# Layer 0 holds its 192 channels as 128 and 64 instead of 96 and 96

## The chip, the cores and the metric

The kernel runs on one core of one Trainium2 chip. The metric is the device time of one launch in microseconds. The core has TensorE (matmuls, into PSUM), VectorE, ScalarE, GpSimd and SyncE, which issues the DMAs; each has its own queue of instructions, and they wait for one another by semaphores.

## The reference

The input x is 16 images of 56x56 tokens with 192 channels, fp32. Layer 0 is a window attention block and an MLP:

```
xn = layernorm(x) * ln1_w + ln1_b, rolled by (-3, -3), in windows of 7x7 tokens
q, k, v = xn @ qkv_w + qkv_b              # 6 heads of 32 channels, 49 tokens a window
o = softmax(q k^T / sqrt(32)) v           # per window and head
x = x + roll back(o @ proj_w + proj_b)
x = x + gelu(layernorm(x) @ mlp_w1 + mlp_b1) @ mlp_w2 + mlp_b2      # 192 -> 768 -> 192
```

Layer 1 is a selective scan in four directions over the image, with 192 channels and 16 states, and a LayerNorm at the end. The change does not touch it.

## The kernel before

`build` runs four blocks one after the other: `build_layer0`, `build_prep` (projections of the scan), `build_scan` and `build_output`. The change is in `build_layer0` and in the layout of one table of per-channel constants (`cols0`).

Layer 0 works in 128 units. A unit is one row of 8 windows of an image: 8 x 49 = 392 tokens. The loop over units is software pipelined: `step(u)` does the attention of unit u and the MLP of unit u - 1. Each engine has its own program of the step, in a fixed order written out by hand, and waits on semaphores that count units and pieces.

Tokens stand on partitions in two places (x and LayerNorm, in tiles of 98 tokens, `PT`, of which there are four, `NPAIR`); elsewhere channels stand on partitions. The 192 channels are held as two halves of 96 (`HC`), index a, on the partitions 0 to 95: `xnT[96, 2, ...]`, `qkT[96, 4, 392]`, `oT`, `h2T`, `x1T`, and the weights as `[96, 2, ...]`. So each product over channels is two accumulated matmuls of 96 rows with 392 tokens as columns (192 for v and proj).

TensorE's order in `step`:

1. q and k (L436): four pieces of 96 channels into PSUM banks 6 and 7 in turn, each waiting until ScalarE (L336) has copied the piece two before it.
2. LayerNorm 2's transposes of unit u - 1 (L375, `norm2_transposes`), once VectorE has made x-hat (L200). ScalarE applies scale and shift (L289, `affine`).
3. v (L447): four pieces into banks 6 and 7, copied by VectorE (L242).
4. `mlp_in` (L398): six pieces of 128 hidden channels into banks 6 and 7, each followed by a gelu on ScalarE (L306); at the end ScalarE loads its exp table (L308).
5. `pair_scores` (L422): q times k for a pair of windows, 12 matmuls of 32 rows and 49 columns, into banks 0 to 2 or 3 to 5. The pairs 0 and 1 come first, the pairs 2 and 3 after a third of `mlp_out` each. VectorE takes the maximum (L213), subtracts it (L215), and after ScalarE's exp (L345) sums (L221), inverts and scales (L225).
6. `mlp_out` (L407) for the channel half a = 0 in three thirds, with the residual x2 added by an identity matmul (L411).
7. For each pair: transposes of the probabilities (L471) into banks 2 and 3, one third of `mlp_out` for a = 1, and the weighted sums of v (L482) of the pair before. Between them VectorE copies the transposed probabilities to SBUF (L254, L255); the banks are single, so the transposes of the next pair wait for this copy.
8. LayerNorm 1's transposes for the next unit (L375), and after ScalarE's copy of the attention output (L352, `oT`) the projection (L497). VectorE adds the residual (L262, `x2`), which starts LayerNorm 2.

ScalarE's order is: rstd of LayerNorm 2, q and k copies (with the rstd of LayerNorm 1 after the third), `affine` for h2T, six gelus, four exps, `result` (x1T, L319 to L322), `oT`, `affine` for xnT. SyncE loads the next unit's x and stores x1T to the DRAM tensor `scr_x` with one DMA (L144). GpSimd adds the projection's bias to x (L177).

The prep stage, of which the prediction uses rows, computes 192 channels as 128 and 64: two full matmuls (L695), then two of 64 rows, one on the partitions 0 to 63 (L697), one on 64 to 127 (L699), into different banks. The scan sums with two matmuls of 64 columns (L1014) into the two partition halves of one bank.

Of the kernel before, what the change touches and what calls it, by code (L numbers as in the profile page):

```python
# [15 lines left out]
ACT = mybir.ActivationFunctionType  # L16
# [15 lines left out]
NPAIR = UW // 2  # L32
HID = 4 * C
# [19 lines left out]
def build_layer0(nc, io, xn, n_units):  # L53
    x_win, w_qkv, w_proj, w1, w2, cols0, b1c, pb, ident = io
    with ExitStack() as ctx:
# [20 lines left out]
        xnT = sb("xnT", [HC, 2, UW, WP])  # L76
        qkT = sb("qkT", [HC, 4, UT])
# [6 lines left out]
        oT = sb("oT", [HC, 2, UT])  # L84
        x2 = sb("x2", [PT, NPAIR, C])
        h2T = sb("h2T", [HC, 2, UT])
        g_sb = sb("g_sb", [128, MC, UT])
        x1T = sb("x1T", [HC, 2, 2, UT])
# [5 lines left out]
        LN1W, LN1B, QKB, VB, LN2W, LN2B, B2 = 0, 2, 4, 8, 10, 12, 14  # L94
# [12 lines left out]
        s_full = sem("a_s_full")  # L107
# [21 lines left out]
        def _(sp):  # L129
            for dst, src in ((wqkv_sb[:], w_qkv.rearrange("(a p) n -> p a n", a=2)),  # L130
                             (wp_sb[:], w_proj.rearrange("(a p) n -> p a n", a=2)),
                             (w1_sb[:], w1.rearrange("(a p) n -> p a n", a=2)),
                             (w2_sb[:], w2.rearrange("(a p) n -> p a n", a=MC)),
# [27 lines left out]
            def last(u, half, par):  # L161
                sp.wait_ge(x1_done, 2 * u)
                store(u - 1, 1 - par)
                sp.wait_ge(x1_out[0], 16 * half + 16)
                sp.wait_ge(x1_out[1], 16 * half + 16)
# [4 lines left out]
        def _(pool):  # L170
            pool.wait_ge(w_in, 16 * 8)
# [11 lines left out]
        def _(dve):  # L183
            nc.vector.memset(ps[:, 0:6, :], 0.0)
            nc.vector.memset(xnT[:], 0.0)
            nc.vector.memset(eps_sb[:], LN_EPS).then_inc(ready, 1)
# [43 lines left out]
            def step(u, half, par, first, is_last):  # L230
# [1196 lines left out]
```

## Time and profile before

| | us |
|---|---|
| median of 3 runs | 23417.88 |
| lowest and highest run | 23393.66 and 23420.24 |
| the profiled execution | 23412.67 |
| its span | 23410.9 |
| PE busy in the span | 17671.3 (75%) |
| DVE busy | 19513.2 (83%) |
| ACT busy | 9356.7 (40%) |
| POOL busy | 16923.9 (72%) |

Layer 0 takes the first 5360 us of the span, the prep stage lies behind it until about 7850 us, then come the scan and, at the very end, the output. The shares of the whole span are means over these stages: in layer 0 GpSimd does almost nothing, in the scan VectorE and GpSimd are busy nine tenths. In a timeline of the profile neighbouring instructions of one line are merged into one row with their number; a time in brackets is the engine's idle time before the row and what ended it.

### The profile page before, as it was taken

What the parts mean: (1) busy time and instruction counts of PE and PEld (TensorE: products, weight loads), DVE (VectorE), ACT (ScalarE), POOL (GpSimd) and SP (SyncE); (2) the same over time, 40 slices, a digit from 0 to 9 for tenths busy, and PEclk for the clock granted to TensorE, in tenths of its full rate; (3) what the DMA queues carried; (4) which work ended last, traced back from release to release, by engine and by line L of the source; (5) the groups of instructions that cost most, each with busy time, mean ns of one, the idle gap of its engine ahead of it and who ended that gap; (6) DMA issues with size and microseconds to landing.
All of it is one profiled execution on the core that took longest, in us unless ns stands there. A gap on an engine that the chain in (4) does not pass through costs nothing. (4 is left out here: it accounts for less than half of the span.)

```text
span 23410.9 us, 290956 instructions
## 1 busy us (share of the span) xinstructions
PE 17671.3 (75%) x83608; PEld 6368.3 (27%) x83608; DVE 19513.2 (83%) x21619; ACT 9356.7 (40%) x14503; POOL 16923.9 (72%) x9092
## 2 busy tenths in 40 slices
PE   8999999997777677777777777777777777777731
PEld 5556555552222111111111111111111111111111
DVE  5555555556666899999999999999999999999976
ACT  3333333334444344444444444444444444444420
POOL 0000000007888899999999999999999999999977
PEclk9999999998777676777677677767766776677665
DMA  0000000004555555555555555555555555555556
GB/s 17 15 15 14 14 14 14 14 14 148 184 178 181 140 118 121 119 122 117 116 121 122 121 116 118 122 121 120 118 117 120 121 122 117 116 121 122 119 135 166
DMA packets 918185, 2417.28 MB, mean 103 GB/s; under 512 B 61030, under 2 KB 270440, under 8 KB 901680
## 3 DMA queue, kind: packets, MB, share of 16 engines
q1 hardware_dynamic: 917040, 2404.95, 45.2%
q8 instruction: 360, 5.90, 0.1%
q14 instruction: 785, 6.43, 0.1%
HBM read 1897.33 MB, written 507.38 MB: 103 GB/s over the span
## 5 line engine op out<-in xcount | busy, mean ns | idle before, releaser
L1162 POOL TENSOR_TENSOR c_pr<-c_hs,c_c_u 128x784 f32<-128x784 f32 x6144 | 11216.7, 1847 | 749.4 <-DVE c_hs L1126 749.4
L1069 ACT ACTIVATE c_psum<-c_dt_u,c_a_neg 128x784 f32<-128x784 f32 x6144 | 5641.6, 918 | 8506.4 <-DVE c_hs L1126 8458.7
L1014 PE MATMUL c_psum<-c_pr,c_red 128*64 128x392 f32 x24576 | 7519.3, 728 | 0.0
L1126 DVE TENSOR_TENSOR_SCAN c_hs<-c_psum,c_carry,c_dbx 128x784 f32<-128x784 f32 x3456 | 6272.7, 1845 | 0.0
L1003 PE MATMUL c_psum<-c_br_u,c_sel 48*128 48x512 bf16 (+1 forms) x9216 | 3210.5, 441 | 3994.8 <-DVE c_dbx L1106 3888.7
L1106 DVE TENSOR_TENSOR c_dbx<-c_u_u,c_psum 128x784 f32<-128x784 f32 x4608 | 4390.2, 953 | 55.4 <-PE c_psum L1003 55.4
L177 POOL TENSOR_TENSOR a_xpb<-a_x_sb,a_pb_sb 98x768 f32<-98x768 f32 x128 | 231.0, 1804 | 5059.8 <-DVE a_x L262 5048.7
L1151 POOL TENSOR_TENSOR c_dbp<-c_u_u,c_bp_u 128x784 f32<-128x784 f32 x1536 | 2858.7, 1861 | 45.0 <-DMA c_c_u<-scr_bc 45.0
L1003 PEld LDWEIGHTS c_psum<-c_br_u,c_sel 48*128 48x128 bf16 x9216 | 557.3, 102 | 8494.5 <-DVE c_dbx L1106 7963.1
L1014 PEld LDWEIGHTS c_psum<-c_pr,c_red 128*64 128x64 f32 x24576 | 1807.9, 181 | 3522.1 <-issue 2286.9
L1126 DVE TENSOR_TENSOR_SCAN c_hs<-c_psum,c_carry,c_dbp 128x784 f32<-128x784 f32 x1152 | 2133.1, 1852 | 0.0
L1126 DVE TENSOR_TENSOR_SCAN c_hs<-c_psum,c_dbx 128x784 f32<-128x784 f32 x1152 | 2018.9, 1782 | 18.6 <-issue 18.6
L407 PE MATMUL a_psum<-a_g_sb,a_w_sb 128*96 128x392 f32 x3072 | 1165.8, 502 | 0.7 <-ACT a_g_sb L306 0.7
L695 PE MATMUL p_psum<-p_xm,p_wk 128*128 128x392 f32 x1536 | 913.6, 724 | 333.7 <-ACT p_xb L726 323.6
L213 DVE TENSOR_REDUCE a_mx<-a_psum 128x6 f32<-128x294 f32 x512 | 234.2, 457 | 1028.2 <-PE a_psum L422 1028.2
L813 POOL TENSOR_SCALAR p_cap<-p_xb 128x784 f32<-128x784 f32 x384 | 988.7, 2575 | 139.6 <-ACT p_xb L726 106.4
L398 PE MATMUL a_psum<-a_h2T,a_w_sb 96*128 96x392 f32 x3072 | 1045.0, 497 | 20.7 <-DVE a_v_sb L242 16.5
L825 POOL TENSOR_TENSOR p_u_o<-p_dt_o,p_xm 128x784 f32<-128x784 f32 x384 | 786.0, 2047 | 237.8 <-DMA scr_u<-p_u_o 208.6
L436 PE MATMUL a_psum<-a_xnT,a_wqkv_sb 96*96 96x392 f32 x2048 | 748.8, 508 | 90.8 <-ACT a_qkT L336 88.3
L790 DVE SCALAR_TENSOR_TENSOR p_psum<-p_m_t,p_psum 128x784 f32<-128x784 f32 x384 | 375.7, 978 | 509.2 <-ACT p_psum L746 496.6
L254 DVE COPY a_pT<-a_psum 49x384 f32<-49x384 f32 x512 | 280.3, 547 | 617.2 <-PE a_psum L471 617.2
L306 ACT ACTIVATE a_g_sb<-a_psum,a_b_sb 128x392 f32<-128x392 f32 x768 | 450.8, 587 | 766.4 <-PE a_psum L398 766.4
(104 smaller groups left out, 17976.1 us busy)
## 6 DMA issues: line engine op xcount, KB each, us to landing
c_c_u<-scr_bc SPq DMA_DIRECT2D x512, 1568.0 KB, 26.9
c_dt_u<-scr_dt SPq DMA_DIRECT2D x512, 588.0 KB, 7.4
c_u_u<-scr_u SPq DMA_DIRECT2D x512, 588.0 KB, 10.8
c_bp_u<-scr_bc SPq DMA_DIRECT2D x512, 392.0 KB, 20.2
scr_dt<-p_dt_o SPq DMA_DIRECT2D x128, 1176.0 KB, 9.6
scr_u<-p_u_o SPq DMA_DIRECT2D x128, 1176.0 KB, 7.2
scr_y<-c_y_sb SPq DMA_DIRECT2D x256, 294.0 KB, 14.4
d_yin<-scr_y SPq DMA_DIRECT2D x32, 2352.0 KB, 14.4
```

The lines of the kernel that those rows point to most:

```text
L398: mm = pe.matmul(ps[:, 6 + m % 2, 0:UT], w1_sb[:, a, 128 * m:128 * m + 128], h2T[:, a, :], start=(a == 0), stop=(a == 1))
L407: pe.matmul(ps[0:HC, 6 + a, 0:UT], w2_sb[:, m, HC * a:HC * a + HC], g_sb[:, m, :], start=(m == 0), stop=False)
L695: pe.matmul(bank(k, h), wk[:, o, 0, m0:m0 + 128], order(xm[:, par, 0, :], o, c, h, HT), start=True, stop=False)
L813: nc.gpsimd.tensor_scalar(cap[:, j % 2], xb[:, n_of(c, j) % 4], CLAMP, None, ALU.min).then_inc(cap_done, 1)
L825: nc.gpsimd.tensor_tensor(u, dt, order(xm[:, par, k, :], o, c, 0, CT), ALU.mult).then_inc(u_done, 1)
L1003: mm = pe.matmul(b_ps[:, n0:n1], sel[:, s % NPR, :], br_u[:, d, n0:n1], start=True, stop=True)
L1014: mm = pe.matmul(Y(3 * w + q)[64 * h:64 * h + 64, :], red[:], pr[:, s % RP, HT * h:HT * h + HT], start=(p == 0 and opens(w)), stop=(p == N ...
L1069: nc.scalar.activation(dA(s), dt_u[:, d, s // NPR, :], ACT.Exp, scale=a_neg[:, k, s:s + 1]).then_inc(exp_done, 1)
L1106: nc.vector.tensor_tensor(dbx[:, (MULS * w + i) % RB, :], u_u[:, d, s // NPR, :], b_ps, ALU.mult).then_inc(mul_done, 1)
L1126: nc.vector.tensor_tensor_scan(hs[:, s % RH, way], dA(s)[:, way], data, init, ALU.mult, ALU.add).then_inc(scan_done, 1)
L1151: nc.gpsimd.tensor_tensor(dbp[:, (len(POOL_STEPS) * w + i) % RG, :], u_u[:, d, s // NPR, :], bp_u[:, d, POOL_PAIRS.index(s % NPR), :], ALU ...
L1162: nc.gpsimd.tensor_tensor(pr[:, s % RP, :], hs[:, s % RH, :], c_u[:, d, s % NPR, :], ALU.mult).then_inc(prod_done, 1)
```

## The change

The 192 channels are held as 128 and 64. The first 128 stand on all partitions, for 392 tokens. The other 64 stand twice: for tokens 0 to 195 (f = 0) on partitions 0 to 63, for tokens 196 to 391 (f = 1) on partitions 64 to 127; these are the new tiles `xnL`, `qkL`, `oL`, `h2L`, `x1L` of 196 tokens. The last 64 rows of the weights are loaded to both partition halves. Products with 128 channels are written as two matmuls of 196 tokens (f = 0, 1) into two banks, followed by two of 64 rows, one for each partition half. Products that make the other 64 channels write partitions 0 to 63 for f = 0 and 64 to 127 for f = 1 of one bank.

The heads 0 to 3 lie in the first 128 channels, the heads 4 and 5 in the rest. `pair_scores` does the heads 0 to 2, then waits for them by the new semaphore `s_half`, then does the heads 3 to 5. The q and k pieces go to banks 4, 5 and 6, v to banks 2 and 3 at once, `mlp_in` to the bank pairs 6, 4 and 6 (`GATE`) with one signal to ScalarE for two gelus. The transposes of the other 64 channels are plain identity matmuls, two passes each. The store is four DMAs, of which three have short pieces (28, 25 and 3 tokens).

```diff
-LN1W, LN1B, QKB, VB, LN2W, LN2B, B2 = 0, 2, 4, 8, 10, 12, 14
+LN1W, LN1B, QB, KB, VB, LN2W, LN2B, B2 = 0, 2, 4, 6, 8, 10, 12, 14
+part = lambda f: slice(WP * f, WP * f + WP)
+cut = lambda f: slice(UH * f, UH * f + UH)
+halved = lambda bank, k: ps[:, bank:bank + 2, cut(k)]
+GATE = (6, 4, 6)
...
+    for tile, w in ((wqkv_sb, w_qkv), (wp_sb, w_proj), (w1_sb, w1)):
+        sp.dma_start(tile[:, 0, :], w[0:128]).then_inc(w_in, 16)
+        sp.dma_start(tile[0:64, 1, :], w[128:C]).then_inc(w_in, 16)
+        sp.dma_start(tile[64:128, 1, :], w[128:C]).then_inc(w_in, 16)
...
+        dst = xrow[:, bass.ds(u * UT + SHIFT * IMG, UT)]
+        sp.dma_start(dst[0:128], x1T[:, par]).then_inc(x1_out[par], 16)
+        low = dst[128:C].rearrange("p (i c) -> p i c", i=WS)
+        lows = x1L[:, par].rearrange("p (i c) -> p i c", i=WS)
+        mid, end = IMG // 2, IMG // 2 - SHIFT
+        sp.dma_start(low[:, :, SHIFT:SHIFT + mid], lows[0:64]).then_inc(x1_out[par], 16)
+        sp.dma_start(low[:, :, SHIFT + mid:IMG], lows[64:128, :, 0:end]).then_inc(x1_out[par], 16)
+        sp.dma_start(low[:, :, 0:SHIFT], lows[64:128, :, end:mid]).then_inc(x1_out[par], 16)
...
+        dve.wait_ge(v_full, u + 1)
+        if not first:
+            dve.wait_ge(av_full, u)
+        for f in range(2):
             for w in range(2):
+                ins = nc.vector.tensor_copy(v_sb[:, HW * f + w:HW * f + HW:2, :],
+                                            ps[WP * w:WP * w + WT, 2 + f, 0:2 * C].rearrange("p (e c) -> p e c", e=2))
+        ins.then_inc(v_evac, 1)
         if not first:
             dve.wait_ge(pt_full, NPAIR * u)
...
+    def affine(dst, low, bank, wcol, bcol, done):
+        for a, (to, n) in enumerate(((dst, UT), (low, UH))):
+            ins = nc.scalar.activation(to, ps[:, bank + a, 0:n].rearrange("p (w k) -> p w k", k=WT), ACT.Identity,
...
     def gelus(u):
         for m in range(MC):
-            act.wait_ge(h_full, MC * u + m + 1)
-            nc.scalar.activation(g_sb[:, m, :], ps[:, 6 + m % 2, 0:UT], ACT.Gelu,
+            act.wait_ge(h_full, MC // 2 * u + m // 2 + 1)
+            nc.scalar.activation(g_sb[:, m, :].rearrange("p (f t) -> p f t", f=2), halved(GATE[m // 2], m % 2), ACT.Gelu,
                                  bias=b1_sb[:, m:m + 1]).then_inc(gelu_done, 1)
...
+        act.wait_ge(qk_full, 2 * u + 1)
+        if not first:
+            act.wait_ge(s_full, NPAIR * u)
+        for a, col in ((0, QB), (1, KB)):
+            nc.scalar.activation(qkT[:, a, :].rearrange("p (f t) -> p f t", f=2), halved(4, a), ACT.Identity,
+                                 bias=cols[:, col:col + 1]).then_inc(qk_evac, 1)
+        act.wait_ge(qk_full, 2 * u + 2)
+        for a, col in ((0, QB + 1), (1, KB + 1)):
+            nc.scalar.activation(qkL[:, a, :], ps[:, 6, cut(a)], ACT.Identity,
+                                 bias=cols[:, col:col + 1]).then_inc(qk_evac, 1)
+        if not is_last:
+            rstd_of(0, u + 1)
...
     def transposes(which, bank, done):
         for t in range(NPAIR):
+            pe.transpose(ps[:, bank, PT * t:PT * t + PT], xhat[:, which, t, 0:128], id_sb[0:PT, 0:PT])
+        for t in (0, 2, 1, 3):
+            mm = pe.matmul(ps[part(t // 2), bank + 1, PT * (t % 2):PT * (t % 2) + PT], xhat[:, which, t, 128:C],
+                           id_sb[0:PT, 0:PT], start=True, stop=True)
         mm.then_inc(done, 1)
...
     def mlp_in(u, attn_u):
         pe.wait_ge(h2_done, u + 1)
+        for m in range(0, MC, 2):
+            if m == 0:
                 pe.wait_ge(x2_done, 2 * u + 2)
+                if attn_u is not None:
+                    pe.wait_ge(qk_evac, 4 * attn_u + 4)
+            elif m == 4:
+                pe.wait_ge(gelu_done, MC * u + 2)
+            for k in range(2):
+                w = slice(128 * (m + k), 128 * (m + k) + 128)
+                for f in range(2):
+                    pe.matmul(ps[:, GATE[m // 2] + f, cut(k)], w1_sb[:, 0, w], h2T[:, cut(f)], start=True, stop=False)
+                for f in range(2):
+                    mm = pe.matmul(ps[:, GATE[m // 2] + f, cut(k)], w1_sb[part(f), 1, w], h2L[part(f), :],
+                                   start=False, stop=True)
+            mm.then_inc(h_full, 1)
+    def mlp_out(u, a, third):
...
+        if a == 0 and third == 0:
+            pe.wait_ge(gelu_done, MC * u + MC)
+        for m in (2 * third, 2 * third + 1):
+            if a == 0:
+                pe.matmul(ps[:, 6, 0:UT], w2_sb[:, m, 0:128], g_sb[:, m, :], start=(m == 0), stop=False)
             else:
+                for f in range(2):
+                    pe.matmul(ps[part(f), 7, 0:UH], w2_sb[:, m, 128:C], g_sb[:, m, cut(f)], start=(m == 0), stop=False)
+        if third == 2:
+            if a == 0:
+                for t in range(NPAIR):
+                    mm = pe.matmul(ps[:, 6, PT * t:PT * t + PT], x2[:, t, 0:128], id_sb[0:PT, 0:PT],
+                                   start=False, stop=(t == NPAIR - 1))
+            else:
+                for t in (0, 2, 1, 3):
+                    mm = pe.matmul(ps[part(t // 2), 7, PT * (t % 2):PT * (t % 2) + PT], x2[:, t, 128:C],
+                                   id_sb[0:PT, 0:PT], start=False, stop=(t % 2 == 1))
             mm.then_inc(m2_full, 1)
...
     def pair_scores(u, q):
+        if q == 0:
+            pe.wait_ge(v_evac, u + 1)
+        elif q >= 2:
             pe.wait_ge(sub_done, NPAIR * u + q - 1)
+        f = q // 2
+        for heads in (range(3), range(3, NH)):
+            for w in range(2):
+                tok = PT * q + WT * w
+                for head in heads:
+                    if head < 4:
+                        rows, t, qk = slice(HD * head, HD * head + HD), tok, qkT
+                    else:
+                        lo = WP * f + HD * (head - 4)
+                        rows, t, qk = slice(lo, lo + HD), tok - UH * f, qkL
+                    mm = pe.matmul(score_rows(q, w, head % 3, head // 3), qk[rows, 0, t:t + WT], qk[rows, 1, t:t + WT],
+                                   start=True, stop=True)
+            if head == 2:
+                mm.then_inc(s_half, 1)
+                pe.wait_ge(s_half, NPAIR * u + q + 1)
         mm.then_inc(s_full, 1)
...
     def step(u, half, par, first, is_last):
         pe.wait_ge(xn_done, u + 1)
+        for k in range(2):
+            w = slice(C * k, C * k + 128)
+            for f in range(2):
+                pe.matmul(ps[:, 4 + f, cut(k)], wqkv_sb[:, 0, w], xnT[:, HW * f:HW * f + HW, 0:WT], start=True, stop=False)
+            for f in range(2):
+                mm = pe.matmul(ps[:, 4 + f, cut(k)], wqkv_sb[part(f), 1, w], xnL[part(f), :, 0:WT], start=False, stop=True)
+        mm.then_inc(qk_full, 1)
+        if not first:
+            pe.wait_ge(x2_done, 2 * u - 1)
+        for k in range(2):
+            for f in range(2):
+                pe.matmul(ps[part(f), 6, cut(k)], wqkv_sb[:, 0, C * k + 128:C * k + C], xnT[:, HW * f:HW * f + HW, 0:WT],
+                          start=True, stop=False)
+            for f in range(2):
+                mm = pe.matmul(ps[part(f), 6, cut(k)], wqkv_sb[part(f), 1, C * k + 128:C * k + C], xnL[part(f), :, 0:WT],
+                               start=False, stop=True)
+        mm.then_inc(qk_full, 1)
         if not first:
             norm2_transposes(u - 1)
+        pairs = lambda t, rows, w: t[rows, w:w + 2, :].rearrange("p w k -> p (w k)")
+        for e in range(2):
+            cols_of = slice(C * e, C * e + C)
+            for f in range(2):
+                pe.matmul(ps[:, 2 + f, cols_of], pairs(xnT, slice(0, 128), HW * f + 2 * e), wqkv_sb[:, 0, 2 * C:3 * C],
+                          start=True, stop=False)
+            for f in range(2):
+                mm = pe.matmul(ps[:, 2 + f, cols_of], pairs(xnL, part(f), 2 * e), wqkv_sb[part(f), 1, 2 * C:3 * C],
+                               start=False, stop=True)
+        mm.then_inc(v_full, 1)
...
+                f = (q - 1) // 2
+                for w in range(2):
+                    tok = PT * (q - 1) + WT * w
+                    for head in range(NH):
+                        if head < 4:
+                            at = ps[HD * head:HD * head + HD, 0, tok:tok + WT]
+                        else:
+                            lo, t = WP * f + HD * (head - 4), tok - UH * f
+                            at = ps[lo:lo + HD, 1, t:t + WT]
+                        mm = pe.matmul(at, v_sb[:, 2 * (q - 1) + w, HD * head:HD * head + HD],
+                                       pT[:, (q - 1) % 2, head // 3, head % 3, WP * w:WP * w + WT], start=True, stop=True)
...
+        if not first:
+            pe.wait_ge(x1_done, 2 * u)
         for e in range(2):
+            at = lambda f: ps[0:PT, 6 + f, C * e:C * e + C]
+            for f in range(2):
+                pe.matmul(at(f), oT[:, UH * f + PT * e:UH * f + PT * e + PT], wp_sb[:, 0, :], start=True, stop=False)
+            for f in range(2):
+                mm = pe.matmul(at(f), oL[part(f), PT * e:PT * e + PT], wp_sb[part(f), 1, :], start=False, stop=True)
+                if e:
+                    mm.then_inc(pj_full, 1)
```

## Rows read from the trace of the kernel before

**Rows 1.** The page's slices: granted clock of TensorE, in tenths.

```profile
PEclk9999999998777676777677677767766776677665
```

**Rows 2.** Busy time by stretch: PE, PEld, DVE, ACT, POOL; PEclk, DMA share, GB/s.

```profile
55.30:5289.30 5234.00, 4851.80 (x43346) 3128.68 (x43345) 2635.59 (x7812) 2035.05 (x4032) 227.36 (x126) 0.97 0.05 14
1252.11:1292.80 40.69, 37.39 (x350) 23.97 (x345) 20.90 (x62) 16.11 (x32) 1.80 (x1) 1.00 0.05 15
2001.40:2043.77 42.37, 39.06 (x349) 25.34 (x344) 20.92 (x62) 16.10 (x32) 1.80 (x1) 0.96 0.05 14
2002.94:2006.36 3.42, 3.42 (x12) 3.11 (x12) 0.55 (x1) 0.85 (x2) 0.00 (x0) 0.50 0.02 8
```

**Rows 3.** Waits of TensorE in 200:5200; us in total, times, longest.

```profile
PE a_psum L471 <- DVE a_pT L255: 116.4, 121, 1.0
PE a_psum L482 <- DVE a_pT L255: 87.5, 121, 0.7
PE a_psum L436 <- ACT a_qkT L336: 84.4, 104, 0.9
```

**Rows 4.** Timeline of TensorE, one unit: start, us, what, [idle before].

```profile
1234.01 0.82 PE L422 MATMUL a_psum<-a_qkT 32*49 32x49 f32 x48
...
1243.77 0.83 PE L471 MATMUL a_psum<-a_id_sb,a_prob 128*49 128x128 f32 x6 [0.97 <-DVE a_pT L255]
...
1252.11 0.88 PE L375 MATMUL a_psum<-a_id_sb,a_xhat 98*96 98x98 f32 x8
1253.42 2.84 PE L497 MATMUL a_psum<-a_wp_sb,a_oT 96*98 96x192 f32 x16 [0.43 <-ACT a_oT L352]
...
1259.77 2.88 PE L436 MATMUL a_psum<-a_xnT,a_wqkv_sb 96*96 96x392 f32 x8 [0.87 <-ACT a_qkT L336]
...
1266.63 8.14 PE L398 MATMUL a_psum<-a_h2T,a_w_sb 96*128 96x392 f32 x24 [0.15 <-DVE a_v_sb L242]
1274.70 0.82 PE L422 MATMUL a_psum<-a_qkT 32*49 32x49 f32 x48
```

**Rows 5.** Timeline of TensorE in the prep stage.

```profile
5742.49 1.58 PE L695 MATMUL p_psum<-p_xm,p_wk 128*128 128x392 f32 x4
5744.00 0.59 PE L697 MATMUL p_psum<-p_xm,p_wk 64*128 64x392 f32 x1
5744.01 0.59 PE L699 MATMUL p_psum<-p_xm,p_wk 64*128 64x392 f32 x1
5744.43 0.49 PE L697 MATMUL p_psum<-p_xm,p_wk 64*128 64x392 f32 x1
...
5744.86 1.59 PE L695 MATMUL p_psum<-p_xm,p_wk 128*128 128x392 f32 x4
```

**Rows 6.** Timeline of TensorE in the scan.

```profile
12001.40 0.88 PE L1014 MATMUL c_psum<-c_pr,c_red 128*64 128x392 f32 x4
```

**Rows 7.** Timeline of VectorE in that unit of layer 0.

```profile
1234.64 0.47 DVE L213 TENSOR_REDUCE a_mx<-a_psum 128x6 f32<-128x294 f32 x1 [8.09 <-PE a_psum L422]
...
1236.49 0.46 DVE L221 TENSOR_REDUCE a_sm<-a_prob 128x6 f32<-128x294 f32 x1
...
1242.62 0.54 DVE L254 COPY a_pT<-a_psum 49x384 f32<-49x384 f32 x1
...
1244.64 0.55 DVE L254 COPY a_pT<-a_psum 49x384 f32<-49x384 f32 x1 [1.01 <-PE a_psum L471]
...
1256.30 0.56 DVE L262 TENSOR_TENSOR a_x<-a_xpb,a_psum 98x384 f32<-98x384 f32 x1 [0.74 <-PE a_psum L497]
...
1259.33 1.25 DVE L200 TENSOR_SCALAR a_xhat<-a_x,a_mv,a_rstd 98x192 f32<-98x192 f32 x4 [0.70 <-ACT a_rstd L283]
```

**Rows 8.** Timeline of ScalarE there.

```profile
1234.11 0.59 ACT L306 ACTIVATE a_g_sb<-a_psum,a_b_sb 128x392 f32<-128x392 f32 x1 [0.73 <-PE a_psum L398]
...
1236.01 0.94 ACT L345 ACTIVATE a_prob<-a_prob 128x294 f32<-128x294 f32 x2
```

**Rows 9.** DMA queues in 1200:1300: packets, MB, share of 16 engines.

```profile
q1 hardware_dynamic: 1842, 1.81, 6.7%
```

More of the change, by code:

```diff
@@ L32 @@
 NPAIR = UW // 2
+HW = UW // 2
+UH = UT // 2
 HID = 4 * C
@@ L163, in last @@
                 store(u - 1, 1 - par)
[L164 to L165 removed]
+                sp.wait_ge(x1_out[0], 64 * half + 64)
+                sp.wait_ge(x1_out[1], 64 * half + 64)
             units(sp, step, last)
@@ L373, in transposes @@
                 for t in range(NPAIR):
-                    for a in range(2):
-                        mm = pe.transpose(ps[0:HC, bank + a, PT * t:PT * t + PT], xhat[:, which, t, HC * a:HC * a + HC],
-                                          id_sb[0:PT, 0:PT])
+                    pe.transpose(ps[:, bank, PT * t:PT * t + PT], xhat[:, which, t, 0:128], id_sb[0:PT, 0:PT])
+                for t in (0, 2, 1, 3):
+                    mm = pe.matmul(ps[part(t // 2), bank + 1, PT * (t % 2):PT * (t % 2) + PT], xhat[:, which, t, 128:C],
+                                   id_sb[0:PT, 0:PT], start=True, stop=True)
                 mm.then_inc(done, 1)
@@ L402, in mlp_out @@
-            def mlp_out(u, a, part):
-                if a == 0 and part == 0:
-                    pe.wait_ge(gelu_done, MC * u + MC)
-                for m in (2 * part, 2 * part + 1):
-                    pe.matmul(ps[0:HC, 6 + a, 0:UT], w2_sb[:, m, HC * a:HC * a + HC], g_sb[:, m, :],
-                              start=(m == 0), stop=False)
-                if part == 2:
-                    for t in range(NPAIR):
-                        mm = pe.matmul(ps[0:HC, 6 + a, PT * t:PT * t + PT], x2[:, t, HC * a:HC * a + HC],
-                                       id_sb[0:PT, 0:PT], start=False, stop=(t == NPAIR - 1))
+                        if attn_u is not None:
+                            pe.wait_ge(qk_evac, 4 * attn_u + 4)
+                    elif m == 4:
+                        pe.wait_ge(gelu_done, MC * u + 2)
@@ L429, in step @@
                 pe.wait_ge(xn_done, u + 1)
-                for e in range(4):
-                    if e >= 2:
-                        pe.wait_ge(qk_evac, 4 * u + e - 1)
-                    elif not first:
-                        pe.wait_ge(x2_done, 2 * u - 1 + e)
-                    for a in range(2):
-                        mm = pe.matmul(ps[0:HC, 6 + e % 2, 0:UT], wqkv_sb[:, a, HC * e:HC * e + HC], xnT[:, a, :, 0:WT],
-                                       start=(a == 0), stop=(a == 1))
-                    mm.then_inc(qk_full, 1)
+                for k in range(2):
[4 more added lines that the diff above has]
+                        mm = pe.matmul(ps[:, 4 + f, cut(k)], wqkv_sb[part(f), 1, w], xnL[part(f), :, 0:WT], start=False, stop=True)
```

151 lines of the change are left out of this document (49 added, 102 removed).

## The prediction

> **What bounds the kernel now.** I read the slices of the page first, then the busy time by stage, then the waits of TensorE, then one unit engine by engine. The slices show TensorE at nine tenths and its clock at nine in the first nine of 40 slices, layer 0, and a lower clock behind [rows 1]. The stage row gives 126 units in 5234 us, so 41.54 us for one, with TensorE busy 93% of it, VectorE 50% and ScalarE 39% [rows 2]. So layer 0 is bound by TensorE. The other three quarters of the time, layer 1, are not touched by the change, and I take them as they are. What TensorE waits for in layer 0 is short but regular: 116 us for the copies of the transposed probabilities in front of L471, 88 for the same in front of L482, 84 for ScalarE in front of L436, over 122 units [rows 3]: 2.4 us a unit.
>
> One unit, from scores to scores, is 1234.01 to 1274.70: 40.69 us at full clock (2.4 GHz) [rows 4]. Another unit took 42.37 us at a mean clock of 0.96; in it a stretch of 3.4 us was granted 0.50, which is 1.2 GHz [rows 2]. So a stretch of 3.4 us at 1.2 GHz costs 1.7 us, and the clock adds 41.54 - 40.69 = 0.85 us to the mean unit.
>
> **Prices.** One pass is one recorded matmul; an fp32 matmul is two passes, a fp32 transpose one. A pass's record is 0.16 longer than its stream (0.49 in the second ones of L697 [rows 5], for 0.33). L398: 24 passes of 392 columns in 8.14 us, less 0.24 for the first load and this end, is 0.329 us each. L497: 16 passes of 192 columns in 2.84, in the same way 0.163 each. A pass of 196 columns is 0.166 by the same slope [rows 4].
>
> The prep stage already has the pattern of the change: two full 128x128 matmuls, then two of 64 rows side by side into two banks. L695 starts at 5742.49, L697 and L699 start 0.01 apart at 5744.00 and 5744.01, their second passes at 5744.43 and 5744.44, and the next L695 at 5744.86 [rows 5]. So the pair does run side by side. A set lasts 2.37 us; its streams are 4 + 2 passes, 6 x 0.329 = 1.97; 0.39 us is left for going into the tiled mode and out. The row starts place it: 5742.49 to 5744.00 is 1.51 for four passes (1.32), 0.19 more; the tiled part is 0.86 for two passes (0.66), 0.20 more. Each change of mode costs about 0.19: the array runs empty (0.09: L398's record ends at 1274.77, its stream at 1274.61, L422 starts at 1274.70 [rows 4]) and the first weights load uncovered (0.10 for 128 columns, 0.05 for 64). Two column halves side by side are in the scan: four passes of L1014, 0.88 us with load and end [rows 6]; one after another they would be 1.3. These prices do not shrink with the matmul, and the change cuts 392 columns to 196. So a set of 128 rows, then 64, costs 6 x 0.166 + 0.39 = 1.38 us.
>
> The Trainium skill (TensorEngine Tiling (Array Packing), Theoretical Speedup and Key Properties) gives "up to 2x" for a dimension of 64 and says that a change of mode drains the array. By the factor alone mlp_in would take 36 x 0.166 = 5.98 us; with the price that the row gives it is 8.3, which is more than now. The trace agrees with the drain and sizes it.
>
> **Part by part, from the norm1 transposes (time 0, 1252.11 now) to the scores.** Now this is 22.59 us.
> - The transposes: 8 passes of 0.085 become 4 of 0.109 (128 weights to load, L471's spacing), a change to 64 columns (0.14) and 4 passes of 0.085: 0.92 for 0.68. It is hidden: L497 waits until 1.31 for ScalarE's two copies L352. These copy 392 and 196 elements instead of twice 392, about 0.2 sooner: proj starts at 1.11.
> - proj: 12 passes of 0.163 and four changes of 0.17 = 2.65 (now 2.68). End 3.76.
> - q and k, 128 channels: two sets, 2.77. End 6.53. Then 64 channels, column pairs, then 64x64 pairs: 8 x 0.166 + 4 x 0.145 = 1.91. End 8.44. Now it is 16 x 0.329 = 5.26 and a wait of 0.87 for ScalarE in the middle [rows 4], which goes, since the four parts have banks that are free.
> - norm2 transposes need x-hat. VectorE's x2 additions begin 0.2 after proj, at 3.96 and 4.42; behind the second one x-hat ends 4.28 after its start (1256.30 to 1260.58) [rows 7]: 8.70. This is late next: TensorE waits 0.35. Transposes 1.03, end 9.83.
> - v: two sets of 192 columns, 2 x 1.365 = 2.73, end 12.56. Now it is 16 x 0.163 = 2.61 and waits for v copies, which go; mlp_in starts at 14.52 (1266.63). The affine h2T is ready at about 12.1, behind LayerNorm 1's rstd on ScalarE; a cover of only 0.4.
> - mlp_in: six sets, 8.30, end 20.86. Now 24 x 0.329 = 7.90. Scores start at 20.95. Sum: 22.59 - 20.95 = 1.64 us gained.
>
> One pair is shown by no row: 64x64 on the diagonal, both into bank 6. Bounds: side by side 0, one after another 4 passes more, +0.66 us a unit. I take 0, nearest to L1014's two halves in one bank, and keep 0.66 for the range. The Trainium skill (TensorEngine Tiling, Gotcha 1: PSUM Pressure) says that different row tiles can't write one PSUM bank at once; by it the sum would be 0.66 x 127 = 84 us worse. No run shows it for different partitions.
>
> **From the scores (time 0, 1234.01) to the norm1 transposes.** Now 18.10 us.
> - Scores: the new wait s_half stands on TensorE between three heads and the next three. The first half must land (0.24 with its load) and its semaphore return (0.1): about +0.35 for each pair. Bounds: 0.2 (a pass of L422 takes 0.20) to 0.6. Queued behind it are the other scores and the MLP's matmuls. For pair 0 VectorE waits: it starts at 0.98 instead of 0.63.
> - The last two gelus come together after mlp_in: ScalarE starts them at 0.1 and ends at 1.17 instead of 0.69; table load 1.28 and exp follow, so exp 0 ends at 2.94 (now 2.45). VectorE's first sum waits for it: 2.98 instead of 2.48 [rows 7, 8]. Softmax on VectorE then runs unbroken and ends 0.50 later, at 9.11.
> - TensorE meanwhile: scores 0 and 1 until 1.2, three thirds of mlp_out for 128 columns (4 x 0.329 each, as now), scores 2 and 3, x2 with 128 columns (8 x 0.109), transposes of the probabilities start at 7.98 and land at 8.85. That is before 9.11: hidden, by 0.26. With s_half at its upper end it would not be.
> - Now a cycle: copies of pT (1.01), 0.14 to TensorE, 0.87 to the next copy (1243.77 to 1244.64) = 2.02. Beside it TensorE has mlp_out for the other 64 columns, 4 x 0.166 + 0.14 = 0.81 instead of 1.32, and the weighted sums, about 0.47. Copies start at 9.11, 11.13, 13.17, 15.55 (before the last, 0.36 more for the x2 part and a change of mode); the last weighted sums at 16.71, the transposes at 17.19. Now the copies are at 8.61, 10.63, 13.21 and 16.46: here the halved L407 gains. Sum: 18.10 - 17.2 = 0.9 us [rows 4, 7].
>
> **Other edges.** VectorE's v copies are 4 instead of 8, hidden under mlp_in. The store becomes four DMAs with 1344 more pieces of 112 bytes or less. 1842 packets took 6.7% of 100 us on 16 engines, 0.058 us each [rows 9]: 84 more per engine are 5 us of a unit's 40, and ScalarE asks for the buffer only two units later. If a small piece cost ten times this, it would decide; I see no sign of it. Six more weight loads delay the start by about 2 us. Added to SP's queue are three issues of 0.3 us, under 40 us of idle.
>
> **Sum.** 20.95 + 17.2 = 38.15 us for 40.69: 2.5 us less, x 127 steps = 318 us. I leave the clock's 0.85 as it is. The profiled execution took 23412.7 (span 23410.9); 23412.7 - 318 + 2 = 23097. The median of the runs is 5 higher: 23102.
>
> **Rivals.**
> 1. The waits keep half. TensorE now has slack in front of VectorE (0.35 at the norm, 0.26 at the softmax, 0.4 at h2T), and s_half, the diagonal pair or a slower load of 128 weights under 196 columns can use it up. For: every cover is thin. Against: the prices come from the same pattern. Half of the gain, 1.25 us a unit, is 159 us: about 23260.
> 2. Slower, by the clock. It fell to 0.50 behind the loosest part of the unit, with weighted sums, transposes and two waits; it came back behind unbroken L497 and L436 [rows 2, 4]. The change thins just this: the halved L407, and gaps of 0.19 at each change of mode, so that a set streams 1.0 of 1.38 us where L398 streams all of it. If it falls in each unit and stays low for three such stretches (3 x 1.7 = 5.1), a unit takes 38.15 + 5.1 = 43.25 instead of 41.54: +1.7 x 127 = +217, about 23630. It decides from 3.4 us of clock cost a unit on, two stretches. Against: the new matmuls use 128 rows instead of 96, and the sets of rows 5 ran at the full rate (1.51 us for four passes and a load).
> 3. The pairs do not run side by side (the change doesn't do what it says). Then 22 pairs of a unit cost two passes of 0.166 more each, 7.3 us: 45.5 instead of 40.69, x 127 = +605, about 24020. Rows 5 and 6 speak against it.
>
> **Chances.** Forecast 0.60, rival 1 0.24, rival 2 0.10, rival 3 0.02, no difference (within 0.2%, 47 us, what a measurement of this kernel can tell from no change) 0.04. The low end: the clock never falls (0.85 more) and a little of the waits goes, 3.5 x 127 = 445: 22970. The high end lies behind rival 1, 23340. Faster 0.84, same 0.04, slower 0.12.
>
> **What would show it.** Sets of mlp_in every 1.38 us, starts of a pair 0.01 apart; mlp_in at 8.3 us, longer than now; scores of a pair about 0.35 longer; softmax starting 0.35 later and pT copies 2.0 apart; a unit at full clock of 38.2; clock of layer 0 near 0.97. Layer 1 unchanged. It is wrong if the clock of layer 0 falls below 0.9, if units are over 40, or if a wait longer than 0.5 stands before mlp_in.

## The result, and the profile after

The changed kernel takes 23267.8 us (median of 5 runs, 23243.6 to 23328.2) where the kernel before takes 23417.9 (5 runs, 23393.7 to 23424.7): ratio 0.994, interval 0.9924 to 0.9955. It is faster by 150 us, 0.6%, which is small but clear of the noise. The forecast was 23102, a gain of 316; so less than half of it came. The profiled execution took 23276.9 (span 23275.0). TensorE ends layer 0 at 5200.1 us instead of 5359.6, 159.5 less, and the rest of the kernel is 23 us longer.

The page's clock row and its row of instruction queue q8 (packets, MB, share of 16 engines); the kernel before had 360 packets there, 5.90 MB:

```profile
PEclk9999999997777666776777677667767776677665
...
q8 instruction: 916, 15.01, 0.3%
```

Busy time by stretch, with the columns of [rows 2]: 120 units, then two units in a row at full clock:

```profile
97.56:4938.05 4840.49, 4496.79 (x48484) 2961.47 (x48482) 2432.64 (x6960) 1734.91 (x3600) 216.85 (x120) 0.96 0.08 17
1074.10:1112.10 38.00, 35.03 (x400) 22.98 (x398) 20.32 (x59) 14.46 (x30) 1.82 (x2) 1.00 0.08 17
1112.10:1152.60 40.50, 37.26 (x412) 24.83 (x412) 20.22 (x58) 14.45 (x30) 1.81 (x2) 1.00 0.08 17
```

A mean unit takes 40.34 us (before 41.54 [rows 2]). At full clock there are two kinds: 38 us, as forecast, and 40.5. They alternate. What stands before the longer one is in the timeline of TensorE (start, us, what, idle before it and what ended that), which answers to [rows 4]:

```profile
1081.58 0.93 PE L428 MATMUL a_psum<-a_h2T,a_w_sb 128*128 128x196 f32 x4
1082.44 0.60 PE L430 MATMUL a_psum<-a_h2L,a_w_sb 64*128 64x196 f32 x4
1082.97 0.93 PE L428 MATMUL a_psum<-a_h2T,a_w_sb 128*128 128x196 f32 x4
...
1089.94 0.67 PE L470 MATMUL a_psum<-a_qkT 32*49 32x49 f32 x13
...
1091.19 1.58 PE L440 MATMUL a_psum<-a_g_sb,a_w_sb 128*128 128x392 f32 x4
...
1107.17 0.56 PE L401 MATMUL a_psum<-a_id_sb,a_xhat 98*128 98x98 f32 x4
...
1108.24 0.89 PE L560 MATMUL a_psum<-a_wp_sb,a_oT 128*98 128x192 f32 x4
...
1113.64 0.93 PE L484 MATMUL a_psum<-a_xnT,a_wqkv_sb 128*128 128x196 f32 x4 [2.68 <-issue]
...
1130.42 0.67 PE L470 MATMUL a_psum<-a_qkT 32*49 32x49 f32 x13
...
1150.88 0.57 PE L562 MATMUL a_psum<-a_wp_sb,a_oL 64*98 64x192 f32 x4
1151.38 0.93 PE L484 MATMUL a_psum<-a_xnT,a_wqkv_sb 128*128 128x196 f32 x4
```

Between proj (L562) and the first q, k matmul (L484) of the next step TensorE stands idle 2.68 us at 1113.64 and none at 1151.38. "issue" says that it waited for no engine and no DMA of the kernel. L484 is the first matmul of a step, and TensorE's loop holds two steps: this is the jump back. Its waits in 200:5000 (us in total, times, longest), beside [rows 3]:

```profile
PE a_psum L484 <- issue: 133.4, 60, 3.0
PE a_psum L549 <- DVE a_pT L276: 85.3, 119, 0.7
PE a_psum L533 <- DVE a_pT L276: 64.0, 119, 0.5
```

The wait for ScalarE in front of q and k (84 us) is gone. In its place stand 60 waits of 2.2 us on average with no releaser.

The queues in 500:4500 explain the first page row: q8 moved nothing there before. Now it moves nine packets of 16 KB for each body, two of them just before the jump's first matmul (447 packets; 4000 us hold 49.6 bodies of 2 x 40.34 us).

```profile
q1 hardware_dynamic: 192657, 59.94, 6.8%
q8 instruction: 447, 7.32, 0.8%
```

So the theory to test: **a body of two steps has grown past what TensorE keeps of its instructions.** A unit has 404 recorded matmuls and as many weight loads instead of 344 (43346 in 126 units [rows 2]), a body of two steps 1616 recorded instructions instead of 1376; if they no longer fit, the target must be loaded anew at each jump back. The rivals: the time is lost in the waits (rival 1), in the clock for reasons of the new code (rival 2), or in the 1344 small pieces of the store.

The Trainium skill (Runtime: NRT & Kernel Launch, Instruction fetch mechanics) gives TensorE room for 2048 instructions, loaded in blocks of 16 KiB with 256 instructions each, and says that a taken branch to a target outside the two blocks held stalls the engine until the target is loaded. The trace agrees with the block (7.32 MB in 447 packets) and with the stall, but not with the two blocks: the body of the kernel before has 1376 recorded instructions, more than two blocks by that page, and jumps back without a load. Here the measurement decides.

### The profile page after: what moved, and what is told of

It is laid out like the page before. It is cut to its first block and busy times, and to the rows that moved or that the text cites. A ratio compares the mean times of both kernels' runs of the same rounds, so it can differ in the third digit from the quotient of the medians.

```text
span 23275.0 us, 306000 instructions
## 1 busy us (share of the span) xinstructions
PE 17560.9 (75%) x91288; PEld 6351.0 (27%) x91288; DVE 19437.2 (84%) x21108; ACT 9140.2 (39%) x14247; POOL 16921.3 (73%) x9092
## 5 line engine op out<-in xcount | busy, mean ns | idle before, releaser
L428 PE MATMUL a_psum<-a_h2T,a_w_sb 128*128 128x196 f32 x3072 | 717.7, 356 | 1.2 <-ACT a_h2L L310 1.2
L328 ACT ACTIVATE a_g_sb<-a_psum,a_b_sb 128x392 f32<-128x392 f32 x768 | 409.4, 584 | 785.9 <-PE a_psum L430 785.9
L1415 PE MATMUL d_psum<-d_id_sb,d_yf 96*112 96x96 f32 x896 | 153.3, 360 | 745.1 <-DVE d_yf L1350 672.3
L1191 DVE TENSOR_TENSOR_SCAN c_hs<-c_psum,c_dbp 128x784 f32<-128x784 f32 x384 | 685.4, 1785 | 0.0
L804 ACT ACTIVATE p_e_t<-p_cap 128x784 f32<-128x784 f32 x384 | 328.7, 856 | 889.8 <-POOL p_cap L878 888.6
```

The lines of the kernel that those rows point to most:

```text
L328: nc.scalar.activation(g_sb[:, m, :].rearrange("p (f t) -> p f t", f=2), halved(GATE[m // 2], m % 2), ACT.Gelu, bias=b1_sb[:, m:m + 1]).th ...
L428: pe.matmul(ps[:, GATE[m // 2] + f, cut(k)], w1_sb[:, 0, w], h2T[:, cut(f)], start=True, stop=False)
L1191: nc.vector.tensor_tensor_scan(hs[:, s % RH, way], dA(s)[:, way], data, init, ALU.mult, ALU.add).then_inc(scan_done, 1)
```

## The experiments

"Mean unit" is that over some 120 units, "full" a unit at full clock (2.4 GHz) without a jump, "low" the time at 1.2 GHz in a mean unit; these three columns are in us and from the profiled execution.

| kernel | median us | ratio to before (interval) | mean unit | full | low |
|---|---|---|---|---|---|
| before | 23417.9 | | 41.54 | 40.63 | 2.3 |
| after | 23267.8 | 0.994 (0.9924 to 0.9955) | 40.34 | 37.93 | 3.1 |
| after_body1 | 23011.5 | 0.9828 (0.9814 to 0.9841) | 38.18 | 37.9 | 0.6 |
| before_body1 | 23417.4 | 1.0001 (0.9992 to 1.001) | 41.55 | 40.63 | 2.3 |
| before_body3 | 23415.9 | 1.0 (0.9991 to 1.0009) | 41.50 | 40.6 | 2.1 |
| after_body3 | 23199.4 | 0.9913 (0.9899 to 0.9926) | 39.66 | 37.9 | 2.8 |
| after_plain_store | 23203.1 | 0.9907 (0.9892 to 0.9922) | 39.66 | 37.9 | 2.2 |
| plain_store_body1 | 23012.1 | 0.9828 (0.9815 to 0.9842) | 38.21 | 37.9 | 0.7 |
| pause_body1 | 23701.4 | 1.0117 (1.0101 to 1.0132) | 43.64 | | 8.7 |
| mlp_grouped | 23029.8 | 0.9831 (0.9817 to 0.9844) | 38.28 | 37.33 | 2.3 |
| all_grouped | 22883.1 | 0.9766 (0.9753 to 0.978) | 37.20 | 36.67 | 1.3 |
| all_grouped_swapped | 22852.2 | 0.9758 (0.9745 to 0.9771) | 36.89 | 36.20 | 1.6 |

### The size of the loop's body

One edit of TensorE's loop alone, with K = 1 or 3 in place of the two steps a body; each step is the same code:

```diff
-            units(pe, step, last)
+            step(0, 0, 0, True, n_units == 1)
+            with pe.Fori(0, (n_units - 2) // K) as i:
+                for j in range(K):
+                    step(K * i + j + 1, 0, 0, False, False)
+            step(n_units - 1, 0, 0, False, True)
+            last(n_units, 0, 0)
```

**after_body1** (the changed kernel, K = 1).

> TensorE's loop holds one unit instead of two; the work and its order are the same. Theory A (instructions): two units of the changed kernel are too many instructions for what TensorE keeps, so they are loaded anew in each iteration, and it stands still some 2.2 us at the jump back, in front of L484. With one unit a body this wait and the instruction packets of the steady state go: 63 x 2.2 = 140 us less and a little of the clock, so 23268 - 140 = about 23110, 0.6% under the changed kernel, ratio to before 0.987. Theory B (the clock and the smaller matmuls take the gain): nothing changes, 23270, ratio 0.994; the wait stays, once a unit.

Measured: 23011.5, 256 us less than after, where theory A expected 158. Its q8 row on the page, a unit's windows, and its two longest waits; there is no "issue" row among them:

```profile
q8 instruction: 345, 5.65, 0.1%
```

```profile
97.17:4678.37 4581.20, 4366.91 (x48484) 2884.42 (x48482) 2432.43 (x6960) 1737.46 (x3600) 216.85 (x120) 0.99 0.07 16
```

```profile
PE a_psum L549 <- DVE a_pT L276: 89.1, 124, 0.7
PE a_psum L533 <- DVE a_pT L276: 65.4, 123, 0.6
```

The matmuls, waits and transfers are those of after (x48484 in both), and the unit is 2.16 us shorter. Instruction loads, stall and longer unit go together. The waits for VectorE are as long as in after, so they are not where the time went. The granted clock is now 0.99 instead of 0.96, which is what theory A had put too low.

**before_body1** (the kernel before, K = 1).

> The kernel before with one unit in TensorE's loop, a control. It has no instruction packets in its steady state and no such wait, so by both theories nothing is gained: 23418, ratio 1.000, within 0.1%. If the jump itself cost something, it would show here as a loss: 63 more jumps.

Measured: the same as before. A small body is no gain by itself; the 256 us belong to the change.

**before_body3** (the kernel before, K = 3: 2064 recorded instructions).

> The kernel before with three units in TensorE's loop: some 2070 recorded PE and PEld instructions in a body instead of 1380; the changed kernel has some 1640 in two units. Theory A: the wait of 2.2 to 2.7 us at the jump now comes to the kernel before, 42 times: +92 to +113 us, about 23520, ratio 1.004, and instruction packets in the steady state. Theory B: 23418, ratio 1.000.

Measured: no change, against the expectation of some 100 us more. The loads are there, and the pause too: the page's q8 row, two rows of TensorE's timeline at a jump, and its waits there in the steady stretch:

```profile
q8 instruction: 764, 12.52, 0.2%
```

```profile
1047.31 2.84 PE L497 MATMUL a_psum<-a_wp_sb,a_oT 96*98 96x192 f32 x16 [0.35 <-ACT a_oT L352]
1051.20 5.17 PE L436 MATMUL a_psum<-a_xnT,a_wqkv_sb 96*96 96x392 f32 x15 [1.05 <-DVE a_x L262]
```

```profile
PE a_psum L436 <- ACT a_qkT L336: 66.7, 84, 0.9
PE a_psum L436 <- DVE a_x L262: 26.4, 23, 1.5
```

The pause puts the first q, k matmul off by 0.9 to 1.5 us (median 1.1) at 24 of the 41 jumps; at the other 17 the proj before it runs at 1.2 GHz, and there is none. Where it comes, the wait of 0.87 us for ScalarE inside q, k [rows 4] is not there: q and k run through (x15). Three units at full clock take 122.16 us instead of 3 x 40.63 = 121.9, so 0.25 more. So the pause was hidden behind a wait, one that the change removes. The expectation failed because it added the pause to a sum and did not ask what it covers, and because it took its size from after: it is 1.1 us here, 2.6 there.

**after_body3** (the changed kernel, K = 3).

> The changed kernel with three units in TensorE's loop. Theory A, if the price is one wait at each jump: 42 waits instead of 63, 21 x 2.2 = 46 us less than the changed kernel, about 23220, ratio 0.9915. If the price went by the instructions loaded, it would be 23268, the same. Theory B: the same too.

Measured: 68 us less than after, where 46 were expected. The longest stall is 2.8 us (3.0 in after), and it stands before every third unit instead of every second. Its row in 200:5000:

```profile
PE a_psum L484 <- issue: 73.1, 37, 2.8
```

The share of units with a pause is a half, a third, none; the time 23268, 23199, 23012. It is the jump that costs. In proportion, the step from a half to a third would be worth 85 us and the one from a third to none 171; 68 and 188 were measured. The five runs of after alone lie 85 us apart, so whether the difference is more than noise is not shown; the low clock fits it (3.1, 2.8 and 0.6 us a unit), and its cost comes below.

### The small pieces of the store

**after_plain_store** leaves the turn of the 64 upper channels into image order out, so that each of their DMAs writes long rows:

```diff
-        sp.dma_start(low[:, :, SHIFT:SHIFT + mid], lows[0:64]).then_inc(x1_out[par], 16)
-        sp.dma_start(low[:, :, SHIFT + mid:IMG], lows[64:128, :, 0:end]).then_inc(x1_out[par], 16)
-        sp.dma_start(low[:, :, 0:SHIFT], lows[64:128, :, end:mid]).then_inc(x1_out[par], 16)
+        sp.dma_start(dst[128:C, 0:UH], x1L[0:64, par]).then_inc(x1_out[par], 16)
+        sp.dma_start(dst[128:C, UH:UH + 98], x1L[64:128, par, 0:98]).then_inc(x1_out[par], 16)
+        sp.dma_start(dst[128:C, UH + 98:UT], x1L[64:128, par, 98:UH]).then_inc(x1_out[par], 16)
```

> The changed kernel, two units in TensorE's loop, with the 64 channels stored in the order of the tile instead of the image's: three DMAs of long pieces instead of 1344 pieces of 12 to 112 bytes a unit. It leaves out the turn into image order for these channels. Theory S (the small pieces stand in front of TensorE's instruction loads on the DMA engines and so make the wait at the jump longer): the wait falls from 2.6 us towards the 1.3 of before_body3, up to 63 x 1.3 = 80 us and part of the clock's price, 23150. Theory A (the wait is the load itself, in its own time): 23268, the same within 0.1%.

Measured: 65 us less than after. The same wait, in 200:4600:

```profile
PE a_psum L481 <- issue: 93.9, 53, 2.2
```

At full clock the pause is 2.0 us instead of 2.6, and the low clock takes 2.2 us a unit instead of 3.1. **plain_store_body1** is the same with K = 1:

> after_body1 (23012) with the store of after_plain_store, which leaves out the turn into image order for 64 channels. Theory S (the small pieces cost only where TensorE's instruction loads stand behind them; after_plain_store gained 65 us with the wait at the jump 2.0 instead of 2.6 us): with no loads there is nothing to gain, 23012 within 0.1%. Rival (the small pieces cost by themselves, in the end of layer 0 or by the DMA of x): 20 to 60 us less here too.

Measured: 23012.1, beside 23011.5 with the small pieces. So they cost nothing of their own, only where instructions are loaded. At the jumps the second packet on q8 starts 2.3 us behind the first instead of 2.6 (medians), while a packet itself takes 0.95 us in both. That the small pieces are in its way on the DMA engines, which both use, is the likely reason; it is not shown.

### A pause without loads

**pause_body1** is after_body1 with one wait more: the first q, k matmul of a step also waits for VectorE's statistics of LayerNorm 2 for the unit before, which come some 2.3 us after proj.

```diff
         pe.wait_ge(xn_done, u + 1)
+        if not first:
+            pe.wait_ge(ln_dve[1], 3 * u - 2)
```

> after_body1 with a pause and no instruction loads: TensorE waits in front of q and k, in each unit, for the first statistics of LayerNorm 2, which end 2.4 us after the projection. It prices what a pause at this place does to the clock. The pause itself: 2.4 - 0.35 of slack at x-hat = 2.05 us a unit, 39.97 at full clock, x 127 = +260, 23272. Theory K (the pause pulls the clock down as the wait at the jump did: 3.1 us at 1.2 GHz a unit with it, 0.6 without it): 0.9 us a unit or more on top, over 23385, and low-clock stretches of over 3 us a unit. Theory N (the clock has nothing to do with it): 23272, mean low clock time 0.6 us a unit as in after_body1.

Measured: 23701.4, 690 us more than after_body1. The wait (total, times, longest), the 120 units, and the clock row of the page:

```profile
PE a_psum L486 <- DVE a_stats L211: 233.5, 101, 2.4
```

```profile
101.76:5341.31 5239.55, 4759.06 (x48480) 3110.57 (x48480) 2432.48 (x6960) 1734.64 (x3600) 216.59 (x120) 0.90 0.06 14
```

```profile
PEclk8989898888777777677767776766776776677665
```

The pause itself is 2.3 us a unit; the unit grew by 43.64 - 38.18 = 5.46. The rest came with the clock: 8.7 us of each unit run at 1.2 GHz, where after_body1 has 0.6. The low stretch lies around the pause: behind it nine tenths of the 128-channel q, k passes run at 1.2 GHz, before it four tenths of the proj passes. No load of instructions is needed for that.

### Fewer changes of mode

**mlp_grouped** (K = 1, like the next two): in mlp_in four full matmuls of two 128-column blocks stand together, then their four of 64 rows; each block has its own pair of banks, and the second pair of scores waits for the last gelu.

```diff
-        GATE = (6, 4, 6)
+        GATE = (6, 4, 0, 2, 6, 4)
...
+            at = lambda k, f: ps[:, GATE[m + k] + f, cut(0)]
             for k in range(2):
-                w = slice(128 * (m + k), 128 * (m + k) + 128)
                 for f in range(2):
-                    pe.matmul(ps[:, GATE[m // 2] + f, cut(k)], w1_sb[:, 0, w], h2T[:, cut(f)], start=True, stop=False)
+                    pe.matmul(at(k, f), w1_sb[:, 0, w_of(k)], h2T[:, cut(f)], start=True, stop=False)
+            for k in range(2):
                 for f in range(2):
...
-        pair_scores(u, 0)
         if not first:
             pe.wait_ge(gelu_done, MC * (u - 1) + 4)
+        pair_scores(u, 0)
+        if not first:
+            pe.wait_ge(gelu_done, MC * (u - 1) + MC)
```

> From after_body1 (23012, unit 37.92 us at full clock): mlp_in does the four full matmuls of two hidden pieces first and then their four of 64 rows, each piece in its own bank pair (banks 6, 4, 0, 2, 6, 4), so it goes into the tiled mode 3 times instead of 6. Theory A (a change of mode costs 0.19 whatever the size, and mlp_in stands on the path): 3 x 0.39 = 1.17 us a unit less, 36.75; x 127 = -149, about 22863. Theory B (the second tiled pair's weights can't be loaded ahead either, 0.10 more for each of its two passes): 3 x 0.19 = 0.57 a unit, about 22940. Theory C (ScalarE's gelus and VectorE's v copies become the bound): under 0.3 a unit, over 22970, and a wait in front of mlp_in's second or third group.

TensorE's timeline of mlp_in, and the scores behind it:

```profile
1218.72 1.59 PE L432 MATMUL a_psum<-a_h2T,a_w_sb 128*128 128x196 f32 x8
1220.25 0.93 PE L435 MATMUL a_psum<-a_h2L,a_w_sb 64*128 64x196 f32 x8
1221.16 1.59 PE L432 MATMUL a_psum<-a_h2T,a_w_sb 128*128 128x196 f32 x8
...
1227.17 0.67 PE L475 MATMUL a_psum<-a_qkT 32*49 32x49 f32 x13 [0.49 <-ACT a_g_sb L328]
```

Two sets in one group take 1221.16 - 1218.72 = 2.44 us, not 2 x 1.39 = 2.78: two changes of mode fewer, 0.17 each. mlp_in is 7.21 us long. Of this 1.15 us, 0.5 go to the new wait for gelu, and the time is 18 us above that of after_body1, since the clock is low for 2.3 us a unit and not 0.6. A real gain on TensorE (a full unit is 37.33 us instead of 37.9), given back. None of the three theories had the clock in it, and why it is lower here was not tried.

**all_grouped** does the same for q, k (one part in banks 2, 3, the 64-channel pieces in 6 and 7) and proj (the second pair of token groups in banks 0, 1):

```diff
-    pe.matmul(ps[:, 4 + f, cut(k)], wqkv_sb[:, 0, w], ...)
+    pe.matmul(ps[:, 4 - 2 * k + f, cut(0)], wqkv_sb[:, 0, w], ...)
...
-    at = lambda f: ps[0:PT, 6 + f, C * e:C * e + C]
+    at = lambda e, f: ps[0:PT, 6 - 6 * e + f, 0:C]
```

> From mlp_grouped: the projection and the q and k pieces are grouped in the same way. The projection starts what follows (x2, LayerNorm 2, the transposes), so its two changes of mode less, 0.35, count in full; q and k lose three changes (0.39 + 0.29), but these end in the wait for x-hat in front of the LayerNorm 2 transposes, which grows by as much, so 0. Theory A: 0.35 x 127 = -44 on mlp_grouped, about 22819. Rival: if q and k stood on the path too, 1.03 a unit, -131, 22732.

Measured: 147 us less than mlp_grouped, where theory A expected 44 and the rival 131. The time is still 64 above the 22819 expected, since mlp_grouped had fallen short. The full unit is 0.66 us shorter (36.67), between the 0.35 and the 1.03 of the two, and the low clock takes 1.0 us a unit less. So how much of q and k stands on the path is not settled.

**all_grouped_swapped** lets the last two blocks of mlp_in change their banks, so that the second pair of scores needs gelu 5, not 6:

```diff
-        GATE = (6, 4, 0, 2, 6, 4)
+        GATE = (6, 4, 0, 2, 4, 6)
...
-            pe.wait_ge(gelu_done, MC * (u - 1) + MC)
+            pe.wait_ge(gelu_done, MC * (u - 1) + 5)
```

> all_grouped (22883) with the last two hidden pieces of mlp_in in the other bank pairs (4, then 6), so that the scores of pair 1, which use banks 3 to 5, wait for the fifth gelu and not for the sixth. In all_grouped TensorE waited 57.1 us over 118 units for the last gelu in front of the scores, 0.48 each. Theory A (this wait stands on the path through softmax): it goes, 0.48 x 127 = -61, about 22820, and the unit at full clock falls from 36.67 to 36.2. Theory B (the first softmax sum waits for exp 0 behind the table load anyway): the wait goes and the unit stays at 36.67, 22883.

TensorE's longest waits; with all_grouped the row `L475 <- ACT a_g_sb L328` had 57.1 us, and here it is gone:

```profile
PE a_psum L560 <- DVE a_pT L276: 85.4, 119, 0.7
PE a_psum L401 <- DVE a_xhat L220: 54.2, 120, 0.5
PE a_psum L544 <- DVE a_pT L276: 51.4, 119, 0.4
```

The full unit is 0.47 us shorter, as theory A expected; the time 31 us, half of what it expected, while the low stretch grew from 1.3 to 1.6 us a unit. It is the fastest kernel here: 22852.2, 2.4% under the kernel before (0.9758, 0.9745 to 0.9771).

## Why the forecast went wrong, by its own steps

**What bounds it, prices, the two parts of a unit: right.** A unit at full clock takes 37.93 us where 38.15 were forecast. A set starts 1.39 after the one before (1081.58, 1082.97; forecast 1.38). mlp_in takes 1089.94 - 1081.58 = 8.36 (8.30), longer than the 7.90 before and paid for by the rest. From the scores to the norm1 transposes it is 1107.17 - 1089.94 = 17.23 (17.2), and proj starts 1.07 behind them (1.11). One place was dearer than it was, and forecast so: the scores, two pairs in 1.25 us instead of 0.75, so 0.25 for each wait on s_half (0.35 forecast, 0.2 to 0.6 the bounds). The diagonal pair of 64x64 (L495, 0.55 us for x4) took as long as the column pair in front of it (L492): two passes' time, not four. So the 84 us by the Trainium skill's rule on one bank (TensorEngine Tiling (Array Packing), Gotcha 1: PSUM Pressure) did not come; the measurement decides. VectorE's and ScalarE's rows, beside [rows 7, 8]:

```profile
1090.77 0.46 DVE L233 TENSOR_REDUCE a_mx<-a_psum 128x6 f32<-128x294 f32 x1 [6.82 <-PE a_psum L470]
...
1099.04 0.54 DVE L275 COPY a_pT<-a_psum 49x384 f32<-49x384 f32 x1
...
1101.05 0.55 DVE L275 COPY a_pT<-a_psum 49x384 f32<-49x384 f32 x1 [1.01 <-PE a_psum L533]
```

```profile
1090.05 1.07 ACT L328 ACTIVATE a_g_sb<-a_psum,a_b_sb 128x392 f32<-128x392 f32 x2 [1.72 <-PE a_psum L430]
...
1092.43 0.79 ACT L373 ACTIVATE a_prob<-a_prob 128x294 f32<-128x294 f32 x2
```

The first max starts 0.83 after the scores (0.98), the pT copies 9.10 after them (9.11) and 2.01 apart (2.02).

**Other edges: no miss that costs.** A small piece adds about 0.011 us of one DMA engine, not 0.058; plain_store_body1 shows that it costs nothing.

**Sum: this is the step that failed.** It reads "20.95 + 17.2 = 38.15 us for 40.69: 2.5 us less, x 127 steps", with the clock's 0.85 left as it is. Two terms are wrong:
- *A term is missing.* The sum counts matmuls by their time and never their number. The body of TensorE's loop went from 1376 to 1616 recorded instructions, and every jump back now stops TensorE for 2.57 us (median at full clock), on half of the units. Full-clock pairs of units average 39.08 us, which is 1.15 more than 37.93: 146 us over 127 steps. No row of before shows such a pause, since q8 moves nothing in layer 0's steady stretch there; only the count of instructions would have raised the question. The forecast had even counted what hides such a pause: the wait of 0.87 us for ScalarE in q, k "goes". before_body3 shows that with it in place a pause of 1.1 us costs 0.25.
- *A term changed.* The clock costs 40.34 - 39.08 = 1.26 us a unit, not 0.85: 52 us over 127 steps. after_body1 has 38.18 - 37.93 = 0.25. So without the pause the new code is better for the clock than the old, not the same.

The two make 198 us of 318; 0.22 us a unit of the other sign (37.93 for 38.15) gives 28 back, and the rest of the kernel takes 23 more. 318 - 198 + 28 - 23 = 125, beside 136 between the two profiled spans. 16 us of the 23 are in the prep stage; it is 14 to 20 us longer in every kernel of the new layout.

**Rivals.** Rival 1 gave the nearest number (23260) by luck and not by its mechanism: no wait for VectorE or ScalarE takes a half of the gain. Rival 2's mechanism is real: pause_body1 is slower than before by it. What it needs is the pause; the changes of mode alone, which it blamed, go with a clock of 0.99 in after_body1; mlp_grouped has fewer of them and more low clock. Rival 3 is out: pairs start 0.01 us apart. Of the signs named as making the forecast wrong, one came true: units over 40 us. No wait over 0.5 us stands before mlp_in, and the clock of layer 0 is 0.96.

The body's part is shown: after_body1, after_body3 and before_body1 change only that. That the pause is a load of instructions is shown by q8's packets. In layer 0's steady stretch they come only in the kernels with a pause at the jump: nine a body in after and after_plain_store, twelve in after_body3 (404 packets in 33.6 bodies), ten in before_body3, none in the others. And they time it. At the jump of 1113.64 packets run from 1108.37 to 1109.67 and from 1111.14 to 1112.10, and the first q, k matmul starts 1.54 us after the second has landed. At all 62 jumps of after that distance is 1.5 to 1.7 us, while the pause itself goes from 0.6 to 3.0; in before_body3 it is 1.6 to 1.8 at all 24 jumps with a pause.

The size of what TensorE holds is placed by the runs only between 1376 and 1616 recorded instructions. An estimate by the Trainium skill (Runtime: NRT & Kernel Launch, Instruction fetch mechanics): nine blocks of 256 hold at most 2304 instructions, waits and register work included, so a body of after can be longer than the 2048 that the page gives TensorE; no run shows that it is.

**Open:** why two packets, one after the other, stand before the first q, k matmul in after and only one in before_body3, which is why the pause is 2.6 us in the one and 1.1 in the other (the last packet starts 0.2 us behind the last row of proj in the one, in the median, and 1.3 before it in the other); the prep stage's 14 to 20 us; why mlp_grouped has a lower clock; how short a pause leaves the clock alone.

## What to carry to other kernels

Count an edit's instructions as well as its time: when one unrolled body of an engine's loop grows, ask whether it still fits what the engine holds, look for the instruction queue's packets in the steady stretch, and try one unit a body. Before you remove a wait, name what else it hides: a stall that costs nothing behind it shows in full once it is gone. And price a gap on TensorE by two terms, its length and the clock behind it, since the second can be larger.

## What was not expected of the hardware

- A jump back in a body of 1616 recorded instructions of TensorE stalls it for 2.6 us (2.0 with fewer small DMA pieces about), in one of 2064 for 1.1 (kernel before), in one of 2424 for up to 2.8 (after_body3), in one of 1376 or less not at all. Work starts again 1.5 to 1.8 us after a packet of instructions has landed. The packets of a body come all along it, nine to twelve of 16 KB, so more is loaded than the jump's target.
- A gap of 2.3 us in each unit of 38 brings 8.7 us at 1.2 GHz with it in that unit (pause_body1; 0.6 without the gap).
- One change of mode costs 0.17 us by the grouped sets, 0.195 by the sum of rows 5; it is paid by count, so putting sets together takes 1.15 us off mlp_in with the same passes.
- Two 64x64 matmuls on the diagonal of the array write different partitions of one bank side by side (L495: starts under 0.01 us apart).
